# Full attention in one Trainium2 kernel: queries and keys in two 12-bit parts instead of three bfloat16 parts

## What is computed

```python
q = (hidden_states @ Wq.T + bq).reshape(b, s, HEADS, HEAD_DIM)
k = (hidden_states @ Wk.T + bk).reshape(b, s, HEADS, HEAD_DIM)
v = (hidden_states @ Wv.T + bv).reshape(b, s, HEADS, HEAD_DIM)
q = q * SCALE
scores = jnp.einsum('bqhd,bkhd->bhqk', q, k)
probs = jax.nn.softmax(scores.astype(jnp.float32), axis=-1).astype(scores.dtype)
out = jnp.einsum('bhqk,bkhd->bqhd', probs, v).reshape(b, s, d)
return out @ Wo.T + bo
```

## Time and profile before

| what | value |
|---|---|
| median of 3 runs | 2994.47 us (2993.47 to 2994.68) |
| span of the profiled execution, its own time | 3043.6 us |
| PE / PEld / DVE / ACT / POOL busy in it | 2495.8 / 1107.6 / 2292.3 / 1887.0 / 1220.7 us |
| projection and score loop | about 252 to 1029 us |
| exp of the score loop (L1323) | 1024, mean 601 ns |
| maximum of the first pass (L1350) | 512, mean 1219 ns |

### The profile page before, as it was taken

The page is one execution under the profiler, slowest core; times in us unless marked ns, Lnnn a source line. Parts: engine busy times, 40 slices in busy tenths (PEclk is TensorE's granted clock), DMA queues, the critical chain, the costliest instruction groups (busy, mean ns, idle before and its releaser), DMA issues. The chain is left out here.

```text
span 3043.6 us, 43434 instructions
## 1 busy us (share of the span) xinstructions
PE 2495.8 (82%) x13082; PEld 1107.6 (36%) x13254; DVE 2292.3 (75%) x4236; ACT 1887.0 (62%) x3760; POOL 1220.7 (40%) x1394
## 2 busy tenths in 40 slices
PE   6897899999998899969999999895746555565666
PEld 5543222222222444424444444485711111111466
DVE  7777888888888477866666666665369999999843
ACT  2213688888887421326666666414459999999743
POOL 2015434433335101638888888704522020200054
PEclk8999899999999999979999999997879999989678
DMA  4002322222233100732222222463221111110122
GB/s 100 1 1 89 93 74 74 74 74 75 74 114 103 45 1 1 257 128 88 87 82 84 85 87 92 140 202 79 56 76 42 43 43 43 45 40 31 46 67 75
DMA packets 193925, 229.11 MB, mean 75 GB/s; under 512 B 55824, under 2 KB 122128, under 8 KB 193248
## 3 DMA queue, kind: packets, MB, share of 16 engines
q1 hardware_dynamic: 158960, 193.15, 20.0%
q0 software_dynamic: 31360, 30.05, 4.0%
q10 hardware_dynamic: 3376, 3.15, 0.4%
HBM read 139.72 MB, written 87.95 MB: 75 GB/s over the span
## 5 line engine op out<-in xcount | busy, mean ns | idle before, releaser
L1350 DVE TENSOR_REDUCE neg_max<-ps 128x1 f32<-128x1024 f32 x512 | 601.9, 1219 | 99.8 <-PE ps L1243 92.1
L1323 ACT ACTIVATE prob<-ps 128x512 f32<-128x512 f32 x1024 | 556.3, 601 | 95.3 <-PE ps L1257 82.1
L2650 DVE TENSOR_REDUCE neg_max<-ps 128x1 f32<-128x1024 f32 x512 | 581.2, 1210 | 13.4 <-PE ps L2444 13.2
L2520 ACT ACTIVATE ps<-ps,neg_max 128x1024 f32<-128x1024 f32 x512 | 557.3, 1089 | 23.0 <-DVE neg_max L2650 22.1
L1530 POOL TENSOR_TENSOR acc<-acc,prob 128x512 f32<-128x512 f32 (+3 forms) x320 | 535.3, 1692 | 64.5 <-PE ps L1624 31.3
L1779 DVE CUSTOM_DVE_ANT_0 ps<-ps,mask_strip 128x512 f32<-128x512 f32 (+7 forms) x512 | 382.4, 776 | 221.7 <-PE ps L1598 221.7
L2444 PE MATMUL ps<-k_stack,q_stack 128*128 128x512 bf16 x1000 | 328.6, 414 | 240.9 <-ACT ps L2520 219.1
L1738 ACT ACTIVATE prob<-ps 128x512 f32<-128x512 f32 (+3 forms) x640 | 270.4, 474 | 210.0 <-PE ps L1612 149.7
L1257 PE MATMUL ps<-q_stack,k_stack 128*128 128x512 bf16 x946 | 293.6, 387 | 12.2 <-DMA k_low<-k_parts 5.1
L1267 PE MATMUL ps<-prob,v 128*32 128x512 f32 x2048 | 281.3, 621 | 3.7 <-ACT prob L1323 0.7
L2444 PEld LDWEIGHTS ps<-k_stack,q_stack 128*128 128x128 bf16 x1024 | 62.4, 99 | 502.2 <-ACT ps L2520 424.2
(11 more groups left out here) (368 smaller groups left out, 3944.2 us busy)
## 6 DMA issues: line engine op xcount, KB each, us to landing
q_stack<-q_parts SPq DMA_DIRECT2D x576, 48.0 KB
k_stack<-k_parts SPq DMA_DIRECT2D x576, 48.0 KB
o_quads<-o_out SPq DMA_DIRECT2D x64, 256.0 KB
v<-v_wide SPq DMA_DIRECT2D x32, 512.0 KB
o_pairs<-o_out SPq DMA_DIRECT2D x64, 256.0 KB
num<-o_pairs SPq DMA_DIRECT2D x8, 2048.0 KB, 8.7
q_parts<-parts SPq DMA_DIRECT2D x24, 384.0 KB, 2.5
k_parts<-parts SPq DMA_DIRECT2D x24, 384.0 KB, 2.7
```

What stands on the lines that cost most here:

```text
L1323: nc.scalar.activation(prob[:, m % RING, :], ps[:, bank(m), :], ACT.Exp).then_inc(exped.sem, 1)
L1350: nc.vector.tensor_reduce(neg_max[:, i.slot(2), m:m + 1], ps[:, first:first + 2, :].rearrange("p b n -> p (b n)"), AX.X, ALU.max, negate=T ...
L2520: nc.scalar.activation(s, s, ACT.Exp, bias=neg_max[:, n % 2, qt:qt + 1], accum_out=sums[:, cols(n * KTS + qt, 1)]).then_inc(summed.sem, 1)
L2650: nc.vector.tensor_reduce(neg_max[:, n % 2, qt:qt + 1], ps[:, first:first + 2, :], AX.XY, ALU.max, negate=True).then_inc(maxed.sem, 1)
```

## The change

It touches the full attention alone (`halved=True`); the other attention blocks keep three bfloat16 parts.

- q and k are split in two parts of 12 significant bits, in the type float32r (4 bytes, of which TensorE multiplies the upper bits). ScalarE writes `upper`, rounded to 12 bits; GpSimd subtracts it from `z`, and what is left fits in 12 bits. One copy and one subtraction each instead of two.
- A head has 2 x 2 x 8 = 32 product rows. They lie twice in the stacks, on rows 0 to 31 and on rows 64 to 95, the first with keys 0 to 511, the second with keys 512 to 1023. `k_stack` is 512 columns wide. `q_low`, `k_low` and `load_low` are gone; SyncE loads both copies (`load_halves`).
- First pass: two matmuls of 32 rows (tiles of 32 x 128, at rows 0 and 64), float32r. Second scores: 34 rows, a tile of 64 x 128, float32r; the order of the 16 tiles is now key tile, query half, key half, so that neighbours lie on different tiles.
- The shift is split in float32r halves, turned by a float32r matmul with an identity, and stored with two DMAs.
- The stores of a group are four of 256 KB (float32) instead of two of 384 KB (bfloat16).
- `clear` no longer fills `q_stack`.

```diff
@@ project_qkv
+    def subtract_upper(eng, g, s):
+        for n in (0, 1):
+            hi_ready.wait(eng, g * 2 + n)
+            eng.tensor_tensor(z[:, s, n, :], z[:, s, n, :], upper[:, s, n, :], ALU.subtract).then_inc(lo_ready[n].sem, 1)
...
-                nc.scalar.activation(parts[:, s, n, 0, :], z[:, s, n, :], ACT.Copy).then_inc(hi_ready.sem, 1)
+                if halved:
+                    nc.scalar.activation(upper[:, s, n, :].bitcast(F32R), z[:, s, n, :], ACT.Copy).then_inc(hi_ready.sem, 1)
...
-            for n in (0, 1):
-                rest_ready[n].wait(act, g)
-                nc.scalar.activation(parts[:, s, n, 1, :], z[:, s, n, :], ACT.Copy).then_inc(mid_ready.sem, 1)
+            if not halved:
...
+                for n, dst in enumerate((S.q_halves, S.k_halves) if halved else ()):
+                    hi_ready.wait(sp, (b * 2 + s) * 2 + n)
+                    sp.dma_start(dst[b, :, 0, :, s * GROUP:(s + 1) * GROUP], upper[:, s, n, :]).then_inc(parts_out[b][s], 16)
+                    lo_ready[n].wait(sp, b * 2 + s)
+                    sp.dma_start(dst[b, :, 1, :, s * GROUP:(s + 1) * GROUP], z[:, s, n, :]).then_inc(parts_out[b][s], 16)
@@ new
+def load_halves(sp, S, b, h, t, q_rows, k_rows, keys, loaded):
+    q = S.q_halves[b:b + 1, h, :, :, :].rearrange("b a d t -> b (a d) t")
+    sp.dma_start(q_rows[t * TILE_ROWS:t * TILE_ROWS + PRODUCTS, :],
+                 q.broadcast_to([2, 2 * HD, SEQ])).then_inc(loaded, 16)
+    for a in (0, 1):
+        first = t * TILE_ROWS + a * 2 * HD
+        k = S.k_halves[b:b + 1, h, a, :, keys]
+        sp.dma_start(k_rows[first:first + 2 * HD, :],
+                     k.broadcast_to([2, HD, k.shape[-1]])).then_inc(loaded, 16)
@@ attend
-    tiles = [(kt, c) for kt in range(KTS) for c in range(CH)]
+    tiles = [(g, half, c) for g in range(KTS // 2) for c in range(CH) for half in (0, 1)]
...
-                nc.tensor.matmul(ps[:, first, :], q[own, m * P:(m + 1) * P], k[own, 0:GROUP], start=True, stop=True)
-                nc.tensor.matmul(ps[:, first + 1, :], q_low[i.slot(2)][low, m * P:(m + 1) * P],
-                                 k_low[i.slot(2)][low, :], start=True, stop=True).then_inc(s1_mm.sem, 1)
+                for half in (0, 1):
+                    rows = slice(half * TILE_ROWS, half * TILE_ROWS + PRODUCTS)
+                    op = nc.tensor.matmul(ps[:, first + half, :], q[rows, m * P:(m + 1) * P].bitcast(F32R),
+                                          k[rows, :].bitcast(F32R), start=True, stop=True)
+                op.then_inc(s1_mm.sem, 1)
...
-                nc.tensor.matmul(ps[:, bank(n), :], ks[j.slot(4)][:, kt * P:(kt + 1) * P],
-                                 qs[j.slot(4)][:, c * GROUP:(c + 1) * GROUP], start=True,
+                nc.tensor.matmul(ps[:, bank(n), :], ks[j.slot(4)][rows, g * P:(g + 1) * P].bitcast(F32R),
+                                 qs[j.slot(4)][rows, c * GROUP:(c + 1) * GROUP].bitcast(F32R), start=True,
                                  stop=True).then_inc(s2_mm.sem, 1)
...
-                nc.tensor.transpose(ps[0:SHIFT * KTS, MAX_BANK, 0:P // 2].bitcast(BF16),
-                                    shift[:, h.slot(2), :], S.ident_b[:]).then_inc(m_mm.sem, 1)
+                nc.tensor.matmul(ps[0:SHIFT * KTS, MAX_BANK, 0:P], shift[:, h.slot(2), :],
+                                 S.ident_r[:], start=True, stop=True).then_inc(m_mm.sem, 1)
...
-                if 2 <= c + 1 < HEADS:
-                    load_low(pool, Head(0, c + 1))
...
+                    for first in (PRODUCTS, TILE_ROWS + PRODUCTS):
+                        sp.dma_start(qs[h.slot(4)][first:first + SHIFT, :].rearrange("r (q t) -> r q t", t=P),
+                                     shift_rows[0:SHIFT * KTS, h.slot(2), :]).then_inc(shifted[h.slot(2)], 16)
```

More of the change, by code:

```diff
@@ L5 @@
 F32 = mybir.dt.float32
+F32R = mybir.dt.float32r
 BF16 = mybir.dt.bfloat16
@@ L908, in project_qkv @@
     z = sb("z", [P, 2, 2, GROUP])
-    parts = sb("parts", [P, 2, 2, PARTS, GROUP], BF16)
+    if halved:
+        upper = sb("upper", [P, 2, 2, GROUP])
+    else:
+        parts = sb("parts", [P, 2, 2, PARTS, GROUP], BF16)
     if wide:
@@ L1019, in gpsimd @@
             for s in (0, 1):
[L1020 removed]
+                if halved:
+                    subtract_upper(pool, b * 2 + s, s)
+                else:
+                    subtract(pool, b * 2 + s, s)
             ahead.gpsimd(pool, b)
@@ L1148, in attend @@
     RING = 8
[L1149 to L1157 removed]
+    LOADS = 16 * (2 * 3 + 1)
+    qs = [sb(f"q_stack{n}", [P, SEQ]) for n in range(4)]
+    ks = [sb(f"k_stack{n}", [P, GROUP]) for n in range(4)]
     vs = [sb(f"v{n}", [P, VW, KTS]) for n in range(4)]
@@ L1166, in attend @@
     loaded = [sem(f"loaded{n}") for n in range(4)]
-    low_loaded = [sem(f"low_loaded{n}") for n in range(2)]
     shifted = [sem(f"shifted{n}") for n in range(2)]
@@ L1264, in weigh @@
                 exped.wait(pe, j.times(NT, 4 * g + 3))
-                for n, (kt, c) in enumerate(groups[g], 4 * g):
-                    quad = (c * 2 + kt % 2) * 32
-                    nc.tensor.matmul(ps[quad:quad + VW, OB, :], vs[j.slot(4)][:, :, kt], prob[:, n % RING, :],
-                                     start=kt < 2, stop=kt >= KTS - 2).then_inc(pv_mm.sem, 1)
+                for n, (_, half, c) in enumerate(groups[g], 4 * g):
+                    quad = (c * 2 + half) * 32
+                    nc.tensor.matmul(ps[quad:quad + VW, OB, :], vs[j.slot(4)][:, :, g + half * KTS // 2],
+                                     prob[:, n % RING, :], start=g == 0, stop=g == KTS // 2 - 1).then_inc(pv_mm.sem, 1)
             def turn_shift(h, j):
```

73 lines of the change are left out of this document (29 added, 44 removed).

## The result

| | before | after |
|---|---|---|
| median, us (range, runs) | 2993.97 (2991.35 to 2994.68, 4) | 3547.84 (3545.23 to 3550.23, 4) |
| profiled span, us | 3043.6 | 3547.7 |
| mean granted clock of TensorE | 0.935 | 0.776 |

The change makes the kernel slower: ratio 1.1852, 95% interval 1.1835 to 1.1869, 554 us. Forecast were 2983 us and a range of 2942 to 3030.

What follows compares the result with a forecast made beforehand. The prediction took TensorE to bound the score loop. Its sum was +6 us in the loop, -6.9 for the k_low wait and -10 for projection and entry, -11 from 2994.5: 2983 us, range 2942 to 3030.

Steps and rivals of the forecast that it cites:

- slot of 0.216 us: Score loop: streaming time of one 512-column matmul, taken from bfloat16 at full clock and kept for float32r.
- The load: Score loop: exposed float32r weight load at each tiling change, taken as 0.140 us from the float32 transpose; bfloat16 0.096.
- the rival of slow loads: Score loop: loads of 0.190 us as in float32, group 2.80, head 11.6, total 3028 us; chance 0.10.
- the loop's own length: Score loop: net +0.1 us a head, +6 us over 62 heads; wrong if heads stand under 10.6 or over 11.1.
- The stream: Score loop: a float32r matmul of 512 columns takes one pass, 0.216 us.
- the rival of a slow stream: Score loop: a float32r slot takes 0.43 us; left outside the range together with no overlap, 0.16.
- Side by side: Score loop: second scores on alternating halves overlap, three needing two slots; rival of no overlap 3139 us, chance 0.02.
- The wait for the copy of the shift: Score loop: TensorE's eleventh second score waits for ScalarE's copy of the shift, +0.21 us a head.
- VectorE's pace: Score loop: a first pass's second pair waits for VectorE's reduction two before, +0.20 us a head.
- k_low: At 978 us: TensorE's 4.24 us wait for this load, and the slow matmuls after it, go: -6.9 us.
- The projection: Before the loop: fewer GpSimd subtractions quicken four normalizations to about 2.2 us, period near 4.9 from 6.23.
- The entry: Loop start: head 0 at 298.5, head 1 at 309 us; -10 us with the projection; wrong if head 1 after 315.

Runs made afterwards that it cites:

- the run with the filling products: The change plus unused TensorE products at the loop's entry, 22 of them behind the wait for head 0's loads: 3101.14 us.
- the bfloat16 copy: The kernel before with the change's tiles in bfloat16 (32 rows in the first pass, 34 alternating in second scores; most products left out): 3409.31 us.
- the filling products ahead of the wait: The change plus unused TensorE products at the entry, 20 of them ahead of the wait for head 0's loads: 3552.05 us, ratio 1.1868.
- its copy with 34 rows: The kernel before with its bfloat16 second scores contracting 34 rows instead of 128, most products left out: 2987.07 us.
- the run with a third buffer: The kernel before with three buffers of low parts instead of two, loaded by GpSimd two heads ahead: 2991.09 us, ratio 0.9997.

## Why the prediction was wrong

**The step that failed** is the first: "TensorE is busy 548.7 of 560 us ... at full clock". The clock was read from the kernel before and carried over to another stream of products as if it belonged to the chip: every slot of 0.216 us in the sum takes it for granted, and in the change a slot took 0.43. The loss splits by the measured heads. A head of the change takes 11.46 us at the full clock (692.86 to 704.32 in GpSimd's timeline of the run with the filling products), 19.8 at half, and 10.77 before: 62 x (19.8 - 11.46) = 517 us are the clock's, 62 x (11.46 - 10.77) = 43 the loop's own. That is 560 together, where the loop grew by 558.

The prediction had no rival with another clock. The Trainium skill (TensorE: Matmul & The Clock Gate, What's actually happening) says that the level follows how busy TensorE has been; by it a loop with TensorE 100% busy gets 2.4 GHz. This trace disagrees: 1160 us of unbroken work at 0.50. What separated the kernels here is how many rows are in use: 32 or 34 on two tiles never raised the level (10 of 10 executions: the change, the bfloat16 copy, 34 rows in both passes, the filling products ahead of the wait), 64 in the second scores and 32 in the first pass, in all heads or in some, raised it in 9 of 13, and 64 in the first pass, or 128 in the second scores, in all (before, its copy with 34 rows, and the runs on 128 rows and on 64 rows in both passes). The queries' added rows are zeros, so every product that they add is zero, and the level rose all the same. What exactly the chip reads, these runs don't tell, and several of these kernels ran once.

**The load** of 128 float32r columns was the term mis-sized in the loop: 0.140 taken, 0.183 measured (0.18 in the row at 709.62), near the 0.190 of the rival of slow loads, whose group of 2.80 and head of 11.6 us come close to the measured 2.77 and 11.46. The Trainium skill (TensorE: Matmul & The Clock Gate, LDWEIGHTS), by which it came to 0.18, agrees with the trace of the run with the filling products. That trace has, beside 0.183 us for 128 columns, 0.093 for the 16 of the shift, 0.8 ns a column:

```profile
L1293 PEld LDWEIGHTS ps<-ident_r,shift x64: 92/93/102, 330.2 to 1109.3; 128*16 128x16 f32 x64
```

The slope from 16 to 32 bfloat16 columns, 0.4 ns, which I set against it, misled. Three loads of 0.043 more are 0.13, and gaps of 0.02 to 0.05 a piece the other 0.09 of 2.77 - 2.55. Even at the full clock the change would have come to about 2994 + 43 = 3037 us, an estimate, somewhat over the range's upper end. What the forecast said of the loop's own length was wrong in size, too: +0.1 us a head forecast, +0.69 measured, and a head of 11.46 us lies over the 11.1 beyond which the prediction called itself wrong on the loop.

**The stream** of one pass was right: at the full clock a first pass of two pairs takes 0.66 = 0.18 + 2 x 0.216 + 0.05, so the rival of a slow stream is out; a stream did take twice the forecast time in the change, by the clock and not by the type. **Side by side** was right: four matmuls in the time of two. **The wait for the copy of the shift**: +0.21 forecast, 0.92 - 0.73 = 0.19 measured. **VectorE's pace**, +0.20, didn't show, since the longer group leaves it room.

**k_low**: the wait went, as forecast, but the price was wrong: -6.9 us in the sum. In the run with a third buffer the loop is 3.2 us shorter, since the shift's store is late at the same place by 2.71 us, and the entry takes 3.4 us back. The prediction priced the wait and asked too little what is late next.

**The projection** was right: 2.18 us for four normalizations (2.2 forecast), period 4.76 (4.9), which fits GpSimd's second subtractions as what slowed them; no run takes them away alone. **The entry** was not: -10 us forecast, head 0 at 302.81 (298.5) and head 1 at 317.54 (309). The step that failed is that stores issue as soon as their data is there. GpSimd's last subtraction ends at 295.7 us, but the fourth sequence's eight stores go out from 296.13 to 301.87, 0.57 to 0.98 us apiece (before, a store took 0.36 to 0.48 us to issue). Their transfers fill the DMA engines (share 0.99 from 300 to 305 us), and head 1's loads stand behind them. Head 1 after 315 us was the prediction's own sign of being wrong on the entry. The loop starts 0.8 us earlier.

## What to carry to other kernels

The clock of the engine that bounds a stage is part of its price: when a change makes the products of TensorE's stage smaller (fewer rows in use), ask whether the stage still gets the full clock, and read the granted clock of the stretch before the durations in it. A loop that only just holds its level shows times in two groups, hundreds of us apart; run it several times before believing one. And a wait that is removed is worth what the next latest thing at that place leaves of it, less what the earlier work costs elsewhere: here 3.2 us of 6.9, and nothing in the total.

## What was not expected of the hardware

- TensorE 100% busy for 1160 us at a granted clock of 0.50 (1.2 GHz), in float32r and in bfloat16, with 32 and 34 rows in use.
- The same instructions run at either level: 560 us at 1.00 in one execution (3101 us in all), at 0.50 in others (3548 us); with 64 rows in one pass, the added ones zeros, it was a matter of chance (3074 to 3106 and 3521 us).
- The level fell within some 3 us of a wait of 0.38 to 0.48 us, in four cases, and in three of them stayed down to the loop's end; like waits did nothing in other places.
- A load of 128 float32r columns takes 0.183 us at 2.4 GHz and 0.285 at 1.2; one of bfloat16 0.096.
